# Everything behind the attention as one block in which each engine has its own order, and reciprocal sums spread by a repeated selection column

## The reference, cut to what matters

```python
x = x + _L0_xattn_ref(_layernorm(x), ctx_2048, ...)      # softmax attention, 16 heads of 128, 1500 keys
x = x + _L0_ffn_ref(_layernorm(x), ...)                  # 8 experts of 176 (top 2) and a shared one of 352
x = x + _L1_xattn_ref(_layernorm(x), ctx_2048, ...)      # linear attention, 16 heads of 16, 64 features
x = x + _L1_ffn_ref(_layernorm(x), ...)                  # 8 experts of 176 (top 2), a shared one of 704, gated
```

## Time and profile before

| what | value |
|---|---|
| median of 3 runs | 1333.47 us (1332.1 to 1333.48) |
| the profiled execution, span of the core | 1333.7 us |
| TensorE busy | 1208.5 us, 91% |
| DVE / ACT / POOL busy | 886.9 / 735.6 / 533.6 us |
| mean granted TensorE clock | 0.960 of full speed |
| from the first instruction behind the attention (1047.5 us) to the end | 286.2 us, TensorE busy 222.7 |
| DVE idle at a barrier: ahead of layernorm 1 / 2 / 3 | 1.1 / 1.8 / 1.1 us |
| PE idle for the query weights of the readout | 4.6 us |
| from the last product of `widen(16)` to the end of the second mixture | 9.1 us |
| issue to landing of the second mixture's last weights | 19.5 us |
| granted clock falls, after PE's last product at 1100.1 / 1182.0 us | 4.8 / 1.6 us later |

### The profile page before, as it was taken

How to read it: one execution, slowest core, us unless ns; L and a number is a source line. 1 busy time by engine, 2 the same in 40 slices (tenths; PEclk the granted TensorE clock), 3 DMA queues, 4 the chain that set the end, 5 groups by cost and what they waited for, 6 DMA issues and landing times. The chain is left out here.

```text
span 1333.7 us, 27107 instructions
## 1 busy us (share of the span) xinstructions
PE 1208.5 (91%) x9559; PEld 1043.7 (78%) x9559; DVE 886.9 (67%) x1854; ACT 735.6 (55%) x1263; POOL 533.6 (40%) x554
## 2 busy tenths in 40 slices
PE   5999999999969999999999999999999587967897
PEld 4888888888748888888888888888888475844685
DVE  5656666566557788887888778888775665434543
ACT  4655565556536666566665666666665215412542
POOL 2432232323234463544635446354451334420451
PEclk9999999999979999999999999999999697978798
DMA  4111111110042011110111101100000510005000
GB/s 147 62 41 54 39 54 31 39 39 1 2 113 72 1 47 48 33 60 0 46 46 32 60 0 46 46 32 14 0 1 1 185 55 1 1 20 196 1 1 14
DMA packets 38746, 56.03 MB, mean 42 GB/s; under 512 B 3058, under 2 KB 37154, under 8 KB 38178
## 3 DMA queue, kind: packets, MB, share of 16 engines
q1 hardware_dynamic: 37874, 54.23, 12.8%
q10 hardware_dynamic: 816, 1.05, 0.2%
HBM read 54.81 MB, written 0.46 MB: 41 GB/s over the span
## 5 line engine op out<-in xcount | busy, mean ns | idle before, releaser
L1192 POOL TENSOR_TENSOR att_sq<-att_work,att_sq 128x500 fp32r<-128x500 f32 x90 | 120.4, 1338 | 159.7 <-DVE att_sq L1092 159.7
L1196 POOL TENSOR_TENSOR attention_kk<-att_work,attention_kk 128x500 fp32r<-128x500 f32 x90 | 122.1, 1357 | 153.0 <-DVE attention_kk L1100 153.0
L101 PE MATMUL att_csum<-att_pT,att_cn 125*128 125x448 f32 x384 | 156.5, 407 | 5.3 <-DVE att_pT L1141 4.6
L1018 ACT ACTIVATE att_pr<-att_pr,att_nmx 112x1500 f32<-112x1500 f32 (+1 forms) x96 | 108.5, 1130 | 72.1 <-DVE att_nmx L1129 72.1
L103 PE MATMUL att_csum<-att_pT,att_cn 125*128 125x448 f32 x384 | 141.1, 367 | 0.0
L102 PE MATMUL att_csum<-att_pT,att_cn 125*128 125x448 f32 x384 | 140.2, 365 | 0.0
L1141 DVE TENSOR_TENSOR att_pT<-att_ring,att_pT 125x448 fp32r<-125x448 f32 x192 | 118.2, 616 | 21.5 <-ACT att_pT L1034 21.3
L609 DVE SCALAR_TENSOR_TENSOR attention_kk<-kvs_keys_ps,kvs_bk,attention_kk 64x500 fp32r<-64x500 f32 x96 | 70.8, 738 | 92.0 <-ACT attention_kk L493 90.4
L1126 DVE TENSOR_SCALAR_CACHE_REDUCE att_pr<-att_ring 112x500 f32<-112x500 f32 x192 | 121.8, 675 | 6.2 <-PE att_ring L103 4.8
L364 PE MATMUL kvs_feat<-kvs_f,attention_kk 128*125 128x256 f32 x768 | 113.5, 285 | 10.3 <-DVE kvs_kp L681 10.1
L951 PEld LDWEIGHTS att_ring<-all_ident,att_pr 112*125 112x125 f32 x768 | 110.7, 190 | 14.4 <-ACT att_pr L1018 2.2
(11 more groups left out here) (282 smaller groups left out, 3281.8 us busy)
## 6 DMA issues: line engine op xcount, KB each, us to landing
attention_raw_t<-in_ctxT SPq DMA_DIRECT2D x45, 500.0 KB, 4.1
att_raw_n<-in_ctx SPq DMA_DIRECT2D x16, 750.0 KB
w_gate<-in_gate SPq DMA_DIRECT2D x1, 2112.0 KB, 9.7
w_up<-in_up SPq DMA_DIRECT2D x1, 2112.0 KB, 14.3
kvs_raw_q<-in_wq SPq DMA_DIRECT2D x8, 256.0 KB, 4.0
wo_raw<-in_wo SPq DMA_DIRECT2D x4, 512.0 KB, 6.6
w_down<-in_down SPq DMA_DIRECT2D x1, 2048.0 KB, 18.4
w_gate<-in_gate SPq DMA_DIRECT2D x1, 1760.0 KB, 13.3
```

The lines of the kernel that those rows point to most:

```text
L101: nc.tensor.matmul(out, w_lo, x_hi, start=start, stop=False, skip_group_check=True)
L1018: nc.scalar.activation(pr[:, j, keys], pr[:, j, keys], ACT.Exp, scale=-1.0, bias=nmx[:, j:j + 1], accum_out=z[:, 4 * u + j, c:c + 1]).then ...
L1192: nc.gpsimd.tensor_tensor(sq[1][:, i % 2, :], work[:, i % 2, :], sq[0][:, i % 2, :].bitcast(F32), ALU.subtract).then_inc(sq_lo, 1)
L1196: nc.gpsimd.tensor_tensor(kk[:, c, 2 + gi, :], work[:, i % 2, :], kk[:, c, gi, :].bitcast(F32), ALU.subtract).then_inc(k_lo, 1)
```

## The change

All functions behind the attention are replaced by classes (`Norm`, `AttentionOutput`, `Mixture`, `Readout`) that only hold pieces of work, and by `tail`, one `Phase` with one block, in which each engine's stream is written out. There is no barrier in it. PSUM is one tile of 8 banks that the stages share. The weights of both mixtures use the same SBUF tiles, so SP issues the second one's loads when POOL has read the last block of the first one.

The pieces change too:
- The reciprocals are transposed once, split into high and low halves stacked in 128 rows (`stack`), and for each of the 8 columns of a batch PE multiplies them by one column of a selection matrix (`pick`), repeated 128 times by a stride of zero: 8 products of 112 columns for each batch, with no diagonals.
- The low halves of odd batches and of `Wo`'s quarters 1 and 3 go to POOL.
- Layernorms 1 and 3 go tile by tile. The copies and high halves out of PSUM are of 112 tokens each.
- The membership tables are made in place by POOL, twice (`set_member(pool, 0)` and `(pool, 1)`).
- In the mixture `spread(n)` stands right behind `widen(n)`, and `narrow(n - 2)` behind it. The ranking is three operations over all tiles. Blocks 11 to 13 of the first mixture, units of the shared expert alone, are no longer weighted.
- In the readout the feature products use 32 rows each, ReLU is shared between ACT and DVE, the division covers two batches, the projection is interleaved by tiles, and POOL adds the bias.
- The store is 4 transfers of one tile each.

```diff
+    def spread(self, pe, b):
...
+        for j in range(NJ):
+            n = b * NJ + j
+            last = nc.tensor.matmul(self.bank[:, 2 * (b % 2) + j // 4, j % 4 * TP:(j % 4 + 1) * TP],
+                                    self.pick[:, n:n + 1].to_broadcast([128, 128]), self.stack[:],
+                                    start=True, stop=True, skip_group_check=True)
+        last.then_inc(self.spread_done, 1)
...
+    def tensor(self, pe):
+        self.widen(pe, 0)
+        self.widen(pe, 1)
+        self.turn_weights(pe)
+        self.spread(pe, 0)
+        self.spread(pe, 1)
+        for n in range(2, self.blocks):
+            self.widen(pe, n)
+            self.spread(pe, n)
+            self.narrow(pe, n - 2)
+        self.narrow(pe, self.blocks - 2)
+        self.narrow(pe, self.blocks - 1)
...
+            r = slice(32 * (j % 4), 32 * (j % 4 + 1))
+            nc.tensor.matmul(self.bank[:, self.Q_BANKS[j], 0:NTOK], self.fmap[r, :], self.qT[r, j // 4, :],
+                             start=True, stop=True).then_inc(self.f_done, 1)
...
+        @block.tensor
+        def _(pe):
+            wo.turn_sums(pe)
+            for b in range(4):
+                wo.spread(pe, b)
+            for t in range(TT):
+                for i in range(4):
+                    wo.project(pe, t, i)
+                    if t == 0 and i == 3:
+                        wo.spread(pe, 4)
+                        wo.spread(pe, 5)
+                    if t == 1 and i == 1:
+                        wo.spread(pe, 6)
+                        wo.spread(pe, 7)
+                if t >= 1:
+                    ln1.turn(pe, t - 1)
+            pe.wait_ge(wo.scaled, 2 * B)
+            ln1.turn(pe, TT - 1)
+            for t in range(TT):
+                moe0.logits(pe, t)
+            moe0.tensor(pe)
+            for t in range(TT):
+                ln2.turn(pe, t)
+            lin.query(pe)
+            lin.features(pe)
+            for b in range(4):
+                lin.read(pe, b)
+            for t in range(TT):
+                lin.turn(pe, t)
+                lin.project(pe, t)
+                if t + 2 < TT:
+                    lin.read(pe, 2 * t + 4)
+                    lin.read(pe, 2 * t + 5)
+                if t >= 2:
+                    ln3.turn(pe, t - 2)
...
+        @block.gpsimd
+        def _(pool):
+            wo.set_pick(pool)
+            wo.weights_low(pool, nc.gpsimd, 1)
+            wo.low(pool, nc.gpsimd, 1)
+            wo.weights_low(pool, nc.gpsimd, 3)
+            wo.low(pool, nc.gpsimd, 3)
...
+            moe0.set_member(pool, 0)
+            wo.low(pool, nc.gpsimd, 5)
+            pool.wait_ge(wo.odd_lo, 3)
+            moe0.set_member(pool, 1)
+            pool.wait_ge(moe0.member_done, 2)
+            wo.low(pool, nc.gpsimd, 7)
...
-            attention_output(nc, x, a["x"], qT, rz, a["wo0"], ident, before, w0)
-            layernorm_transposed(nc, "ln1", x, xnT, ident, xn)
-            mixture(nc, "moe0", x, xnT, xn, w0, before, ident, False)
...
+        tail(nc, a, out, ident, kv, qT, qT_at, rz)
```

1282 lines of the change are left out of this document (728 added, 554 removed).

## The result

The changed kernel takes 1311.53 us as the median of 4 runs (1307.69 to 1312.7), against 1332.97 before: the ratio is 0.984, with a 95% interval of 0.982 to 0.985. Forecast were 1301 us and a range of 1291 to 1312. So the sign and the range held, the range by half a microsecond, and the point was 10.5 us too low: 21 us were won where 32 were forecast. The profiled execution is the one at 1307.69, span 1306.0 us, the fastest of the four.

The account below looks back on a forecast made before the run. PE was taken to bound the two mixtures, chains of dependent steps and barriers the other six windows (128.8 us). Eight terms summed to -32.4 us from the 1333.7 us span: 1301.3, as a median 1301 us, range 1291 to 1312.

Parts of the forecast that it names:

- A: Output product, 52.6 us: diagonals and PE's waits go, POOL's low halves then decide; -5.6 us (-10 to -1).
- B: First layernorm, 10.5 us: three tiles done below the projection, two barriers and a table load gone; -5.1 us (-6 to -3).
- F: Third layernorm, 10.9 us: as in the first layernorm, 5.2 us left; -5.7 us (-7 to -3).
- C: First mixture, 71.5 us: block stays 4.44 us, shorter ranking and end, longer wait ahead of spread(0); -1.9 us (-4 to +1).
- D: Second layernorm and wait for query weights, 13.9 us: barriers go, weights already in SBUF; -5.9 us (-7 to -4).
- E: Readout, 32.4 us: feature products overlap at four row positions, projection interleaved, clock falls with gaps; -4.0 us (-8 to 0).
- G: Second mixture, 85.9 us: as the first mixture, with all blocks weighted; -2.0 us (-4 to +1).
- H: End, 8.5 us: two last additions, no barrier, only the last quarter of the output to store; -2.2 us (-3 to -1).
- The POOL rival: Output product gains only 1 us as PE waits on POOL, readout's row positions don't overlap: 1310 us, chance 20%.
- The clock rival: PE's clock holds through the shorter layernorm gaps, so mixtures, output product and readout gain more: 1293 us, chance 20%.
- ends slower: The mixtures' new order starves PE, each steady block grows and the kernel ends slower than before: 1341 us, chance 2%.
- It doesn't do what it says: PE's stream behind the attention stays a chain; only layernorms and end win their barriers, output product nothing: 1325 us, chance 4%.

Follow-up runs that it names:

- The new order: Changed kernel, but in the output product low half 6 and high halves 6, 7 precede layernorm pieces, and PE turns tile 1 inside projection 3: 1300.63 us.
- the first combination: Changed kernel plus the new order, third layernorm in pairs, first three blocks' weights split ahead in both mixtures, widen(2) ahead of spread(0): 1298.70 us.

## Why the prediction was right, and where it was wrong

**Faster by over 0.2%, at 0.97: right**, and for the reason given, that everything outside the two mixtures was bound by chains and not by PE: 20.8 of the 26.4 us were won there. The range held the time at its upper edge; that it was inside by 0.5 us, where the same kernel measured again gave 1308.59, is luck. Some 2 us of the miss are no stage's: they come from setting the profiled span equal to the median of the runs.

**A was wrong**, at the sentence "What now decides is POOL". Its durations were near (2.93 to 3.07 us for a low half beside DVE, 2.08 alone, 2.4 for a quarter), but its start times hung on ACT, and the profile after shows POOL idle when the last tile was needed. What decided was the order on three engines: the layernorm's pieces for tiles 0 and 1 stood ahead of low half 6 on DVE, ahead of high halves 6 and 7 on ACT, and ahead of projection 3 on PE. I had shown that order and costed no place of it: the term "tile 3 starts at 1087.5" came out near the true 1089.3 by another route, which is luck. The new order is worth 4.8 us of the stage and 8 of the kernel; the column alone takes 9.1 from the stage, which was forecast at 5.6 for the whole. The change gained more than I thought there, and lost most of it by its own order.

The end was mis-sized too: the projection ended at 1097, not at 1094.5, because it started 1.8 us later and ran 3.8 us at half clock where 3 were forecast.

**The mutual delay** was in the sum for DVE's operations of 896 elements at 1.1 us each, and was left out for the Newton step ("unchanged, some 2 us"). It hits small operations as hard: 0.15 to 0.16 us alone, 0.46 to 2.07 beside an operation of POOL that reads SBUF. That is 1.3 of B's miss of 1.9 us (its steps at 1099.84, 1100.58 and 1101.45 took 0.71, 0.65 and 0.46), and part of F's. In the first combination, where POOL was idle there, the way from the last addition's end to the router's products is 5.6 us instead of 7.0.

**F was wrong** in "as B". In B three tiles are done below a projection of 5.6 us for each; in F PE needs 1.1 us for a projection, and DVE's chain of some 3.8 us for a tile (addition, statistics, division, low half, Newton step, scaling) is the bound. A per-tile order pays where the tile's own work is longer than the chain. In pairs it gave 1.9 us back.

**C, D, E, G and H** hold in their ends: the wait ahead of `spread(0)` of 2.3 us, the block of 4.44 to 4.45 us, the weights in SBUF in time, the row positions side by side. C's extra 1.4 us and H's 0.7 were not traced further.

**The rivals.** The POOL rival gave 1310, which is nearly the time measured, and neither half of it is what happened: A lost to order and not to POOL's chain, and the rows overlap. A number that fits doesn't show a mechanism. The clock rival, given 20% as "holds" at 1293, asked the right question in the wrong place: I had written of E that with gaps the clock will fall and left it there, while in the executions it falls in some and not in others, for 2.3 us of span between two profiles of the same kernel. What decides it is open. The rival "ends slower" was far off: the steady block didn't grow. "It doesn't do what it says" had B, D, F and H alone win and A nothing; A's small gain looks like it, but its column was worth 9.1.

## What to carry to other kernels

When barriers go and streams are written by hand, each stage's new bound is the order on each engine. Walk the last tile through every engine's list and ask which piece of the next stage stands ahead of what this one still needs; that was 4.8 us of one stage here, with no barrier involved. In the two places seen here, interleaving tile by tile fits only where a tile's matrix work is longer than the small-step chain, else in groups. And measure a part of a bundle alone: the selection column in the old order did better in its stage than the whole rewrite.

## What the hardware showed that I had not expected

- Operations of DVE with one element in a row went from 0.15 us to 0.46 to 2.07 us beside POOL's cuts and subtractions, which read SBUF, and stayed at 0.16 beside its clear; a scaling of 256 elements went from 0.41 to between 1.14 and 1.72 beside a clear.
- The granted clock in the readout differed between executions of one kernel (0.83 and 0.50 in the same 13.7 us), and this is 2.3 us of the spread between its runs. In nine profiles PE was idle for 1.5 to 1.6 us behind the feature products and the clock fell to half soon after; in a tenth, with the new order of the output product, it was idle for 1.53 us and the clock stayed at 1.00. So the gap goes before the fall, but isn't enough for it. With three products that nobody reads in that gap, others in the layernorms' waits, and no wait for ACT, the clock was at 1.00 throughout the readout (1162 to 1189) and the runs agreed within 4.5 us. Fillers in the layernorms' waits of the changed kernel alone gained nothing.
- So PE's shorter work can be worth nothing: with products of 128 rows, 4.3 us longer, the kernel took 1309.05 us where it takes 1308.59 and 1311.53 without.
- Eight products at four row positions took 1.88 us, 3.3 times less than the 6.18 us with all rows. The Trainium skill, "TensorE: Matmul & The Clock Gate", section "Measured speedup vs the span model", gives 3.07 for four row tiles; the case agrees roughly.
